# A decoder's mixture of experts: results scattered to a row per token and rank instead of added up in memory, and slot scatters moved from between the stages into a cross attention

## The reference

```python
x = x + L0_attn(ln(x));  x = x + L0_xattn(ln(x), ctx);  x = x + L0_ffn(ln(x))     # stages A, B, C
x = x + L1_attn(ln(x));  x = x + L1_xattn(ln(x), ctx);  x = x + L1_ffn(ln(x))     # stages D, E, F + experts
```

```python
scores = sigmoid(h @ gate_w.T)                       # 2048 tokens x 32 experts
tki = top 8 of the experts in the 4 best groups of scores + gate_bias
tkw = 2.5 * scores[tki] / sum(scores[tki])
routed = sum over the 8 experts e of tkw[e] * ((silu(h @ w_gate[e].T) * (h @ w_up[e].T)) @ w_down[e].T)
out = x + routed + shared
```

## Time and profile before

| | us |
|---|---|
| runs (3): median, lowest, highest | 3875.18, 3869.48, 3879.73 |
| profiled execution, its own time | 3884.64 |
| its span, first to last instruction | 3882.9 |
| busy: PE, DVE, ACT, POOL | 3455.5, 2416.0, 1803.9, 512.9 |
| mean granted TensorE clock | 0.959 of full speed |
| round 1's stage A to the end of round 4's stage F | 37 to 3501 |
| table and expert blocks to the last scatter | 3501 to 3847 |
| loads of the sums to the end | 3849 to 3883 |

### The profile page before, as it was taken

One profiled execution on the slowest core, in us unless ns is written; L12 is line 12 of the kernel. 1 busy time (PEld: TensorE's weight loads), 2 busy tenths in 40 slices (PEclk: granted clock), 3 DMA queues, 4 the chain that ended last, 5 costly groups with the idle time before them and its releaser, 6 DMA issues.

```text
span 3882.9 us, 62857 instructions
## 1 busy us (share of the span) xinstructions
PE 3455.5 (89%) x21953; PEld 1668.0 (43%) x21953; DVE 2416.0 (62%) x6385; ACT 1803.9 (46%) x3597; POOL 512.9 (13%) x451
## 2 busy tenths in 40 slices
PE   6999989997999889996999889997999889997992
PEld 2352445343362445342352445343352445344772
DVE  5668576854668576853668576853668576853553
ACT  2755434442755434442755434442745434442441
POOL 0000020003000020003000020003000020006885
PEclk9999999998999999998999999998999999997996
DMA  6313001215313001214313001215313201847998
GB/s 211 115 39 64 20 6 48 46 58 157 109 40 63 20 8 46 46 58 150 115 39 64 20 7 47 45 58 167 107 35 61 90 9 46 234 160 172 160 161 172
DMA packets 184288, 317.59 MB, mean 82 GB/s; under 512 B 29972, under 2 KB 139412, under 8 KB 178580
## 3 DMA queue, kind: packets, MB, share of 16 engines
q1 hardware_dynamic: 152888, 270.90, 25.1%
q0 software_dynamic: 29040, 39.86, 5.8%
q10 hardware_dynamic: 2032, 2.61, 0.2%
HBM read 176.94 MB, written 116.70 MB: 76 GB/s over the span
## 4 chain that ended last, share of the span: by engine, by line
PE 68%; DVE 19%; ACT 4%; issue 3%; another core or an unknown queue 3%; DMA 1%; PEldq 1%; SPq 1%; POOL 0%; DVEq 0%; PEld 0%; POOLq 0%; ACTq 0%
PE ps L605 8%; PE ps L588 6%; PE ps L428 5%; PE ps L532 4%; DVE mx L771 4%; PE ps L1860 4%; PE ps L1467 3%; PE ps L593 3%; PE ps L1798 3%; PE ps L484 2%; PE ps L1781 2%; DVE ps L768 2%; PE ps L1757 2%; PE ps L1482 2%
## 5 line engine op out<-in xcount | busy, mean ns | idle before, releaser
L709 ACT ACTIVATE PT<-ps 128x512 f32<-128x512 f32 (+2 forms) x1280 | 643.8, 564 | 332.8 <-PE ps L593 174.6
L771 DVE TENSOR_REDUCE mx<-ps 128x1 f32<-128x512 f32 (+3 forms) x768 | 431.0, 617 | 91.6 <-PE ps L532 49.1
L588 PE MATMUL ps<-QS,KS 99*128 99x512 bf16 (+2 forms) x1280 | 421.1, 370 | 8.5 <-ACT PT L709 8.0
L532 PE MATMUL ps<-KS,QS 96*128 96x512 bf16 (+3 forms) x1280 | 397.1, 373 | 17.5 <-DVE mx L771 7.3
L406 POOL TENSOR_TENSOR rstd<-mv,half 128x4 f32<-128x4 f32 x20 | 20.3, 1016 | 2829.8 <-DVE mv L373 2829.8
L768 DVE CUSTOM_DVE_ANT_0 ps<-ps,mneg 128x512 f32<-128x512 f32 x512 | 340.7, 718 | 82.2 <-PE ps L532 79.0
L605 PE MATMUL ps<-PT,VP 128*32 128x512 f32 (+3 forms) x2560 | 377.1, 577 | 0.0
L428 PE MATMUL ps<-mneg,identb 128*128 128x512 bf16 x1240 | 330.6, 395 | 29.3 <-DVE a_fin L1975 10.9
L588 PEld LDWEIGHTS ps<-QS,KS 99*128 99x128 bf16 x1280 | 108.6, 97 | 395.5 <-ACT PT L709 234.5
L1447 POOL DMA_INDIRECT sums<-wbuf,ctxT x159 | 247.9, 1559 | 57.4 <-issue 37.2
L1975 DVE TENSOR_TENSOR a_fin<-a_fin,ps 128x512 f32<-128x512 f32 (+1 forms) x176 | 104.5, 635 | 210.2 <-PE ps L1840 208.7
(11 more groups left out here) (332 smaller groups left out, 6020.7 us busy)
## 6 DMA issues: line engine op xcount, KB each, us to landing
slot_rows<-in_padrows SPq DMA_DIRECT2D x32, 725.0 KB, 19.8
scores<-a_fin SPq DMA_DIRECT2D x64, 256.0 KB
a_fin<-scores SPq DMA_DIRECT2D x32, 512.0 KB, 4.6
KS<-KP SPq DMA_DIRECT2D x240, 64.0 KB, 2.6
g_xb<-slot_rows SPq DMA_DIRECT2D x105, 145.0 KB
a_Y<-in_wA SPq DMA_DIRECT2D x4, 3072.0 KB, 13.6
scores<-a_fin SPq DMA_DIRECT2D x64, 192.0 KB
a_fin<-scores SPq DMA_DIRECT2D x12, 1024.0 KB, 7.9
```

The source lines that it names most:

```text
L532: last = nc.tensor.matmul(o, m["QS"][0:KR, h, i * P:(i + 1) * P], m["KS"][0:KR, h, f:f + w], start=True, stop=not c.causal)
L588: last = nc.tensor.matmul(o, m["KS"][0:KST, h, j * P:(j + 1) * P], m["QS"][0:KST, h, q0:S], start=True, stop=plain)
L709: nc.scalar.activation(m["PT"][:, mp % 2, j % 2, e, 0:w], ps[:, SLOTS + n % TURNED, 0:w], ACT.Exp, scale=HD ** -0.5).then_inc(g("exp"), 1)
L771: nc.vector.tensor_reduce(m["mx"][:, h % 2, i, f // BANK:f // BANK + 1], ps[:, k % SLOTS, 0:w], AX.X, ALU.max, negate=True).then_inc(g("sl ...
```

## The change

1. **Results.** The accumulating scatter into `sums` becomes a plain one into a new tensor `parts`, which has a row of its own for each token and rank. The row's number travels with the token: behind the 32 weights `xn` now has 32 row numbers, one for each expert (`ROW` = 320). POOL works them out in stage F, a running count over the chosen experts (`f_pool`). The ring `y` has 8 tiles, each with a semaphore. Nothing is zeroed any more.
2. **End.** SP loads `parts` in eight pieces of 2 MB through six buffers (`parts_back`), DVE adds up the eight ranks and adds the row of `x`, which was loaded ahead of block 65 (`kept`), and SP stores a sequence's 512 KB behind each second piece.
3. **Slot scatters.** Those of rounds 1 to 3 are sent in stage B of the next round, one for every three of ACT's exponentials from the 24th on. Those of round 4 are sent in the expert part, 6 ahead and then one ahead of every even block up to block 50. So that `xn` lives until then, stage A's norm writes to another buffer (`xnB`).
4. **Padding.** Pad rows get the new length and rows of their own, and 31 spare blocks (`padtail`) replace one.

```diff
-ROW = DM + 1 + NE + 1
-NACC = 4
+NSPARE = NBLOCK - TOKENS * TOPK // P
+ROW = DM + 2 * NE
...
-                ln_scaled(dve, ch, lambda i: x[:, i, :], ln_pow, n, ln_xn)
+                ln_scaled(dve, ch, lambda i: x[:, i, :], ln_pow, n, ln_xn, xnB)
...
+        def f_pool(pool, ch, n, st):
...
+            nc.gpsimd.memset(m["upto"][:, :, :, 0:half_e], 0.0)
+            ch.link(nc.gpsimd.tensor_tensor(first_part[:, :], first_part[:, :], moeC[:, NE + 18 + NI:NE + 18 + 2 * NI], ALU.add))
+            next_pool(pool)
+            pool.wait_ge(sm["F", "chosen"], 1)
...
+            ch.link(nc.gpsimd.tensor_copy(to[0][:, :, half_e:], m["rp"][:, :, :]))
+            for r, step in enumerate((1, 2, 4, 8, 16)):
+                a, b = to[r % 2], to[(r + 1) % 2]
+                ch.link(nc.gpsimd.tensor_tensor(b[:, :, half_e:], a[:, :, half_e:], a[:, :, half_e - step:half_e + NE - step], ALU.add))
+            ch.link(nc.gpsimd.tensor_tensor(b[:, :, half_e:], b[:, :, half_e:], m["rp"][:, :, :], ALU.subtract))
+            nc.gpsimd.tensor_tensor(xn[:, :, DM + NE:DM + 2 * NE], b[:, :, half_e:], spread(first_part[:, :], 2, [P, NI, NE]), ALU.add)
...
-        RX, RT, RH, RY = 9, 3, 3, 24
+        RX, RT, RH, RY, RB, NB = 9, 3, 3, 8, 6, 8
...
             for b in range(NBLOCK):
                 if b == NFULL:
                     sp.wait_ge(scattered, 16 * B * NI * TOPK)
+                    sp.dma_start(m["kept"], x_kept_rows.rearrange("(t p) d -> p t d", p=P)).then_inc(g("kept_in"), 16)
...
+            def parts_back(q):
+                if q >= RB:
+                    sp.wait_ge(g("summed"), q - RB + 1)
+                rows = TOKENS * TOPK // NB
+                sp.dma_start(m["back"][:, q % RB, :, :], parts[rows * q:rows * (q + 1), :].rearrange("(t p k) d -> p t (k d)", p=P, k=TOPK)).then_inc(g(f"parts_in{q}"), 16)
...
         def g_pool(pool):
             g = lambda s: sm["G", s]
-            pool.wait_ge(x_stored, 16)
-            pool.wait_ge(zeroed, 16 * NACC)
+            for k in range(SLOTS_FIRST):
+                to_slot(k)
             for b in range(NBLOCK):
+                if b % 2 == 0 and SLOTS_FIRST + b // 2 < NI * TOPK:
+                    to_slot(SLOTS_FIRST + b // 2)
                 pool.wait_ge(g("y_up"), b + 1)
-                if b >= NACC:
-                    pool.wait_ge(g(f"added{b % NACC}"), 16 * (b // NACC))
-                nc.gpsimd.indirect_dma_start(out=sums[b % NACC], out_offset=bass.IndirectOffsetOnAxis(ap=token[:, b % RY:b % RY + 1], axis=0),
-                                             in_=MG["y"][:, b % RY, :], in_offset=None, compute_op=ALU.add).then_inc(g(f"added{b % NACC}"), 16)
+                nc.gpsimd.indirect_dma_start(out=parts, out_offset=bass.IndirectOffsetOnAxis(ap=part_row[:, b % RY:b % RY + 1], axis=0),
+                                             in_=MG["y"][:, b % RY, :], in_offset=None).then_inc(g(f"part_out{b % RY}"), 16)
...
                     if b >= RY:
-                        dve.wait_ge(g(f"added{b % NACC}"), 16 * (b // NACC - RY // NACC + 1))
+                        dve.wait_ge(g(f"part_out{b % RY}"), 16 * (b // RY))
...
-            for q in range(B):
...
+            dve.wait_ge(g("kept_in"), 16)
+            for q in range(NB):
+                rows = m["kept"][:, NT // NB * q:NT // NB * (q + 1), :]
+                back = m["back"][:, q % RB, :, :].rearrange("p t (k c) -> p k t c", k=TOPK)
+                dve.wait_ge(g(f"parts_in{q}"), 16)
+                for k in range(TOPK // 2):
+                    last = nc.vector.tensor_tensor(back[:, k, :, :], back[:, k, :, :], back[:, k + 4, :, :], ALU.add)
+                ch.link(last)
+                for k in range(2):
+                    last = nc.vector.tensor_tensor(back[:, k, :, :], back[:, k, :, :], back[:, k + 2, :, :], ALU.add)
+                ch.link(last)
+                ch.link(nc.vector.tensor_tensor(back[:, 0, :, :], back[:, 0, :, :], back[:, 1, :, :], ALU.add))
+                nc.vector.tensor_tensor(rows, rows, back[:, 0, :, :], ALU.add).then_inc(g("summed"), 1)
...
-                    if last and s == "C":
-                        zero_sums(sp)
...
                         a16_pool(pool, ch, CFG[s])
+                        if s == "B" and not first:
+                            for k in range(NI * TOPK):
+                                pool.wait_ge(sm["B", "exp"], EXP_FIRST + EXP_STEP * k)
+                                to_slot(k)
...
-                to_slots(pool)
```

More of the change, by code:

```diff
@@ L270, in decoder @@
         tri = sb("tri", [P, 8, 8])
-        moeC = sb("moeC", [P, 3 * NE + 18 + NI])
+        moeC = sb("moeC", [P, 3 * NE + 18 + 2 * NI])
+        first_part = sb("first_part", [P, NI])
         earlierb = sb("earlierb", [P, P], BF16)
@@ L430, in ln_pe @@
         def ln_pe(pe, n):
+            rows = xnB if STAGES[n] == "A" else xn
             for i in range(NI):
@@ L433, in ln_pe @@
                 for k in range(KD):
-                    last = nc.tensor.transpose(ps[:, k, i * P:(i + 1) * P], xn[:, i, k * P:(k + 1) * P], ident[:, :])
+                    last = nc.tensor.transpose(ps[:, k, i * P:(i + 1) * P], rows[:, i, k * P:(k + 1) * P], ident[:, :])
             last.then_inc(ln_tr, 1)
@@ L1185, in decoder @@
         w_in = [sem(f"w_in{e}_F") for e in range(NSH)]
-        slot_rows = nc.dram_tensor("slot_rows", (NE * ROOM + P, ROW), F32, kind="Internal").ap()
-        sums = [nc.dram_tensor(f"sums{r}", (ROOM, DM), F32, kind="Internal").ap() for r in range(NACC)]
-        padded, zeroed, experts_in = setup_loaded, setup_act, setup_dve
+        slot_rows = nc.dram_tensor("slot_rows", (NE * ROOM + NSPARE * P, ROW), F32, kind="Internal").ap()
+        parts = nc.dram_tensor("parts", (TOKENS * TOPK + (NE + NSPARE) * P, DM), F32, kind="Internal").ap()
+        x_kept_rows = nc.dram_tensor("x_kept_rows", (TOKENS, DM), F32, kind="Internal").ap()
+        padded, experts_in = setup_loaded, setup_dve
         def f_mem(sb2):
@@ L1379, in decoder @@
         MG = scope(g_mem)
-        MG["sum"] = MG["W"][:, :, :].rearrange("p e c -> p (e c)")[:, 0:NACC * NT * DM].rearrange("p (r t c) -> p r t c", r=NACC, t=NT)
+        MG["back"] = MG["W"][:, :, :].rearrange("p e c -> p (e c)").rearrange("p (r t c) -> p r t c", r=RB, t=NT // NB)
         MG["y"] = wbuf[:, :, :].rearrange("p a c -> p (a c)")[:, 0:RY * DM].rearrange("p (r c) -> p r c", r=RY)
-        token = ctxT[:, 0, 0:RY].bitcast(U32)
+        MG["kept"] = wbuf[:, :, :].rearrange("p a c -> p (a c)")[:, RY * DM:(RY + NT) * DM].rearrange("p (t c) -> p t c", t=NT)
+        part_row = ctxT[:, 0, 0:RY].bitcast(U32)
         scratch = ctxT[:, 1, :]
@@ L1394, in x_rows @@
         def x_rows(b):
-            return sums[0][0:TOKENS, :].rearrange("(b t p) d -> p b t d", p=P, t=NI)[:, bass.ds(b, 1), :, :].rearrange("p o t d -> p (o t) d")
+            return x_kept_rows.rearrange("(b t p) d -> p b t d", p=P, t=NI)[:, bass.ds(b, 1), :, :].rearrange("p o t d -> p (o t) d")
         def load_experts(sp, group):
@@ L1400, in load_experts @@
                 sp.dma_start(MG["W"][:, e, :], io["wF"][NSH + e]).then_inc(sm["G", "late_in"] if e in LATE else experts_in, 16)
[L1402 to L1405, removed]
         def pad_experts(sp):
-            sp.dma_start(slot_rows[NE * ROOM:NE * ROOM + P, :], io["padrows"][0:P, :]).then_inc(padded, 16)
+            sp.dma_start(slot_rows[NE * ROOM:NE * ROOM + NSPARE * P, :], io["padtail"]).then_inc(padded, 16)
             for e in range(NE):
@@ L2221, in _, with one_round @@
             st.end_round()
-            with pool.Fori(0, rounds) as b:
+            def one_round(first):
                 ch = Chain(pool, pool_chain)
@@ L2232, in _ @@
                 st.end_round()
-                to_slots(pool)
+            one_round(True)
+            with pool.Fori(0, rounds - 1) as b:
+                one_round(False)
             g_pool(pool)
```

75 lines of the change are left out of this document (40 added, 35 removed).

## The result

The changed kernel takes 3838.9 us (median of 4 runs, 3835.3 to 3843.1) against 3876.4 for the kernel before in the same runs: ratio 0.9903, 95% interval 0.9891 to 0.9916. That is faster and clear of noise, though by less than 1%: 37.5 us where 76 were forecast. The profiled execution has a span of 3841.2 us, 41.7 less than the 3882.9 of before.

What follows compares the result with a forecast made beforehand. PE, busy 89% of the span, bounds the kernel, except at stage A's start, the expert blocks' start and the end. Terms -58 - 23 - 25.5 + 24.5 + 6 = -76: 3875 - 76 = 3799 us; range 3779 to 3857.

Steps and rivals of the forecast that it cites:

- Stage A: Start of stage A, rounds 2 to 4: moving slot scatters out gives back 58 us, bounds 0 and 60.
- Rival 4: Stage A: the loop's jump holds ACT, not the scatters, so stage A returns nothing; 3857 us, chance 0.06.
- Stage B: Stage B takes over 96 slot scatters, one per three exponentials: taken as 0, between nothing and 58 us.
- Stage F: POOL's eight new small operations slow DVE's L378 to L380 beside them: +6 us in four rounds, bounds 0 and 20.
- Start of the blocks: Start of expert blocks: seven slot scatters sent before the first block, first down product 23 us earlier, bounds 0 and 26.
- Blocks: First down product to first return load: cheaper plain scatters, POOL falling slightly behind, 276.6 instead of 302.1 us: -25.5.
- End: After the blocks: eight 2.1 MB return pieces instead of four, taken as 58 us: +24.5.
- my low bound for it, 53.4: End of the kernel: with faster loads DVE's sums would be the bound, 53.4 us.
- The low end of the forecast, -96: Whole kernel: end 53.4, no stall in the blocks, nothing in stage F: -96, 3779 us.
- The first rival: Plain scatters hold ACT wherever dense, 0.61 us each; the 26 among the blocks give +16, 3815 us; chance 0.13.
- The kept rows' load: At block 65: wait for slot scatters, then a 2 MB load before the block's rows: +4.5 us, bounds 0 and 8.

Runs made afterwards that it cites:

- e2: Changed kernel with the 96 slot scatters of rounds 1 to 3 sent at the start of the next round's stage A again; span 3904.1 us.
- e12: e2 with a 128x280 POOL write behind each of its 96 slot scatters; stage A of round 3 takes 67.2 us, where 1.27 us spacing had 87.3.
- e3: Changed kernel with a 128x512 POOL write, waited for, before each scatter of the first 52 blocks; scatters 1.78 us apart, those blocks take 136.8 us.
- e9: Changed kernel, 128x280 write after scatters, 14 slot scatters first, 18 one per three blocks, 12 row buffers, late kept-rows load; last scatter 15.6 us earlier than e8.
- e8: Like e9 but with a smaller write, 128x160; mean scatter spacing 1.56 us, ACT held thirteen times for 1.5 to 2.7 us.
- e7: e3 with a 128x16 write instead of 128x512; scatters 1.38 us apart, ACT held in pieces of 1.9 to 2.7 us.
- e10: Kernel with 1.58 us between scatters, as e9 but its 18 slot scatters one per two blocks; 3810.1 us, ratio 0.9814 to the kernel before.
- e1: Changed kernel with all 32 slot scatters of the last round sent before the first block, none among the blocks; span 3818.2 us.

## Why the prediction was right in sign and half off in size

By its own terms, predicted and measured (profiled executions):

- *Stage A:* -58, measured -58.6. e2 and e12 show the cause. Rival 4 (the loop's jump) is out: ACT still jumps back to stage A in e12 and is hardly held.
- *Stage B:* 0, measured 0. There the scatters are 2.6 us apart on average.
- *Stage F:* +6, measured +4.4; the mechanism is the one named, but most of it fell on L384, which I had left out, and less on L378 to L380.
- *Start of the blocks:* -23, measured -25.5 (first down product at T0 + 20.2 instead of 45.7).
- *Blocks:* -25.5, measured **+25.7**: from the first down product (3460.9) to the first return load (3788.7) are 327.8 us instead of 302.1. This is the step that failed. From the first return scatter to that of block 52 are 134.1 us, where 52 blocks of 1.66 are 86: 48 too many. From there on 188.4, where 106 blocks are 176.
- *End:* +24.5, measured +19.0 (33.5 to 52.5). The sums set the pace, not the loads; my low bound for it, 53.4, was nearly right. (The low end of the forecast, -96, is a slip: the terms that it names add up to -93.)

These make -35.0. The span's -41.7 has 6.7 us more, as much as round 1, in which only stage F changed, was shorter besides (847.9 us for 853.5, with 1.1 added by stage F). That is the difference between executions: round 1 takes 847.9 to 855.5 us in the runs in which its code is equal. The medians differ by 37.5.

The step that failed is the sentence "POOL needs 3 x 1.27 = 3.81 us for two blocks, PE 3.3. It falls 0.25 us a block behind." The arithmetic is right. What it did not ask is what POOL's being behind does to the other engines. The prediction itself had measured it, in stage A and at the start of the blocks: at a scatter every 1.27 us ACT is held. A POOL that has fallen behind sends at just that pace until it has caught up. It had the sign for it, too: "I am wrong if ACT stands in stage B or in the first 52 blocks". I took the accumulating scatters as proof that a stream of scatters in the blocks holds nobody; but those are 1.86 us apart, and e3 at 1.78 shows that side to be harmless. The first rival had the right mechanism and place, and its price was off threefold: 0.61 us for a slot scatter, carried over from stage A, gave +16. What is held is not a scatter's worth, though, but the time until POOL has caught up, in which return scatters count as well as slot scatters. 78 scatters lay in that stretch, not 26, and 78 times 0.61 would have been 48, what was measured.

The kept rows' load cost the 2.8 us for which PE stood, where I had 4.5, and I expected 8 of the experiment from a row of the chain.

The Trainium skill ("Runtime: NRT & Kernel Launch", Instruction fetch mechanics) has a taken branch break the sequential prefetch. I had leant on it to take straight code as safe. Here the straight code of the blocks was held, at their start even before the change, and the code behind the jump was nearly free once the scatters were spaced (e12), so the rule does not tell these cases apart. Nor is the fetch what waits: from 1764 to 1801, while ACT stood in stage A before the change, the trace has no packet on the two queues that carry instructions, and ACT started 0.03 us after PE's late increment.

The Trainium skill ("SBUF — State Buffer", Who interferes with whom) lists forms of tensor_scalar, too, among the DVE operations that can take the port pair that GpSimd uses. L384 is such a form and went from 0.40 to 0.61 us a piece beside POOL: the trace agrees. Reading that list against every DVE line in the stretch would have found the larger part of the cost.

## What to carry to other kernels

Count what an overloaded helper engine does to others, not only how far it falls behind: here POOL's backlog of 0.25 us a block cost PE 0.9 us a block through late signals, since a backlog turns spaced work into back-to-back work. When a hold has been measured in one place, write down its condition (here the spacing) and look for that condition in every stretch of the new schedule, before pricing it by the piece. Look up when the awaited semaphore was raised before calling an engine slow: the engine that stood here was not the one that was late. And a pause can be the fix: with a write of 0.35 us behind each scatter, POOL did more work and the kernel was faster.

## What the runs showed of the hardware

When indirect scatters of 128 rows follow each other fast enough, PE's increments of its semaphores are recorded late, and whoever waits for them stands. Counted are the increments in the 105 us from T0 + 25 (in stage B of round 2 from 1188 to 1270, in the blocks of before from 3600 to 3800), and those recorded over 0.3 us behind the modelled end of the matmul that raised that semaphore last:

```
                                 us apart            PE's increments  late  latest, us
before, blocks, accumulating     1.86                     287           0   0.01
changed kernel, stage B          2.6                      204           0   0.04
e3                               1.78                     122           0   0.01
e9                               1.63 (mean)              143          10   0.9
e8                               1.56 (mean)              141          60   2.7
e7                               1.38                     138          51   4.6
changed kernel, blocks           1.27, in bursts          135          53   4.7
```

ACT's and DVE's increments in the same stretches are never over 0.01 us late. The effect grows as the spacing shrinks rather than setting in at one value; in e12's stage A, at 1.60, a few increments are about 1 us late in rounds 2 and 3 and up to 1.9 in round 4. Single gaps of 1.27 within a slower mean did little harm (e9; e10 has 6 late of 129). The write is not what helps: stage B's scatters and the accumulating ones have none between them. Slot scatters (1280 bytes a row) do it alone (e1's start, e2); return scatters (1024 bytes) alone do it at 1.59, behind e9's last slot scatter (26 of 142 increments late from 3649 to 3749, up to 1.3 us), and were never run alone at 1.27. Whether the spacing itself counts or the number of scatters in flight was not separated: a longer spacing lowers both. Why it is PE's signals that come late stays open.
